# Three shared PSUM bank pairs, neighbour rows worked out on GpSimd, and a one-instruction maximum in a graph and expert kernel

## The chip, the cores and the metric

One core of a Trainium2 chip runs the whole program. The metric is the device time of one execution in microseconds (us). The engines are called as in the profile: PE (TensorE, with its weight loads as PEld), DVE (VectorE), ACT (ScalarE), POOL (GpSimd) and SP (SyncE, which here only issues DMAs).

## What is computed

```python
x = x + gnn(adj, layernorm(x))             # x: 8 x 1024 x 128 f32, adj: 8 x 1024 x 1024 int32
x = x + ffn(layernorm(x), route_id)

def gnn(A, X):                             # S = 25
    scores = where(A != 0, -arange(N), -inf)
    vals, idx = top_k(scores, S)           # the first 25 neighbours of each node
    feats = where(vals > -inf, X[idx], -inf)
    agg = feats.max(axis=2)                # degree <= 25: maximum with 0 too
    return relu(concat([X, agg]) @ W + b)

def ffn(x, route_id):                      # 64 groups of 128 tokens, one of 16 experts for each group
    h = relu(x @ Wi.T + bi)
    for l in range(2):
        h = relu(h @ Ws[l].T + bs[l] + h @ Wr[l, e].T + br[l, e] + h)
    return h @ Wo.T + bo
```

## The kernel before

Each of the 8 batches has 1024 nodes in eight tiles of 128. Tile 0 holds the nodes with the most neighbours (the hubs); it is handled apart. For the seven other tiles (896 target nodes), PE computes for each node how many neighbours came earlier ("rank", L869 and L872, bf16 matmuls of the transposed adjacency with a triangular matrix), ACT copies the rank to SBUF (L641), and then 44 "slots" follow. A slot is a pair (group of source tiles, rank r): an engine makes a one-hot matrix `onehot = (rank == r)` of up to 896 columns (1792 for the group that has two tiles), PE multiplies it with the features (`xsplit`, two parts, L777) into a pair of PSUM banks, and DVE takes the maximum with what is there already (`acc`, a fold, L988; the first two slots of a batch by L986). After 44 folds `acc` holds the maximum over neighbours; L995 merges its two halves.

The slots are numbered p = 0 to 43 in a table. One-hots are shared out by hand: ACT makes 23 of them (by a square and a relu, L670 and L687, or by one relu for r = 1, L681), POOL 16 (L547) and DVE 5 (L975). Six column buffers (`UNITS`) hold them in turn; an engine makes the one-hot of slot p + 5 (ACT, POOL) or p + 4 (DVE) when its own program is at position p, once the buffer's earlier slot has been multiplied.

The program runs in stages s = 0 to 9 of 44 positions, and each engine's instructions are written out by position. In stage s the slots of batch s - 1 run, together with the loading, normalising, mask, transpose and rank work of batch s, and with everything that follows for batch s - 2: the GNN matmuls (p = 2 to 5, L811, L812), the second layer norm (statistics L1169 and norm L1007 to L1018 on DVE, p = 5 to 8; the normalised tile h0 on ACT, L612, p = 9 and 11), turning h0 (PE L819, p = 12 and 13, copied by ACT L618), the first expert matmul (L826, p = 14 to 17), the two expert layers tile by tile (L842 with ACT's relu L629, p = 19 to 34) and the output (L852, p = 36 and 39). In stage 1 the 34 weight matrices are also turned on PE (L908) and summed by DVE (L1153). The steady stages are s = 2 to 7.

PSUM: two pairs of banks for the slots (`slot_ps`), so PE may write slot n when fold n - 2 is done; two single banks for the ranks (`prep_ps`), each used for one half (448 columns) of a rank tile; two single banks (`ffn_ps`) for all that belongs to batch s - 2. The eight ranks of a stage stand at p = 16, 18, 20, 22, 28, 32, 37 and 38.

The hubs: DVE finds each hub's first neighbours by MAX8 and MATCH_REPLACE8 over a `score` row (L1039, L1047, L1049, last at p = 27). At p = 28 DVE turns them into row numbers of a feature table in DRAM (L1057 `spread`, L1058 `floor`, L1061 `idx`); POOL gathers 25 rows for each hub by 25 indirect DMAs (L535), from p = 29 to p = 24 of the next stage; and DVE takes their maximum in two halves of 13 and 12 rows, each in two pieces: one tensor_tensor of six rows with six (p = 14 and 31, L1075 and L1085), and then a chain of four (p = 24 and 34, L1066), with `hub` by L1095.

## Time and profile before

| | |
|---|---|
| median of 3 runs | 740.54 us (737.5 to 740.84) |
| profiled execution | 736.18 us |
| its span in the trace | 734.5 us |
| busy: PE / PEld / DVE | 611.5 / 502.9 / 574.2 us |
| busy: ACT / POOL | 521.2 / 541.9 us |
| granted PE clock, mean | 0.926 of 2.4 GHz |
| chain that ended last | PE 59%, DVE 22%, DMA 4%, ACT 4% |

A batch's first fold (L986) marks the start of its stage: 43.0, 148.0, 225.8, 303.5, 381.5, 459.3, 536.6 and 614.0 us. So stage 1 takes 105 us, the six steady stages some 77.7 us each, the last stage with slots (s = 8) about 76, and the tail some 44. No engine is busy throughout; what has to be read is which of them is waited for at which position of a stage, and that is in the timelines.

### The profile page before, as it was taken

The page shows a single profiled execution, that of the slowest core. Times are in us where ns is not written, and L with a number is a line of the kernel's source. Part 1 is how long each engine was busy: PE and PEld are TensorE (multiplying, and loading weights), DVE is VectorE, ACT ScalarE, POOL GpSimd, SP SyncE. Part 2 cuts the span into 40 slices and gives each one's busy share as a digit, 9 for nine tenths or more (in the row PEclk, how much of TensorE's full clock was granted, in tenths as well). Part 3 has the DMA queues.
Part 4 walks back from the last instruction along what each step waited for, and adds up shares of the span by engine and source line. Part 5 has one row for each costly group of instructions (what it writes and reads, how often), then busy time and mean ns, then how long its engine had stood idle before and what let it go on. Part 6 is the DMA issues. An engine that isn't in the chain of part 4 may idle for free.

```text
span 734.5 us, 11755 instructions
## 1 busy us (share of the span) xinstructions
PE 611.5 (83%) x3496; PEld 502.9 (68%) x3497; DVE 574.2 (78%) x959; ACT 521.2 (71%) x981; POOL 541.9 (74%) x388
## 2 busy tenths in 40 slices
PE   0466666679999799979997999899987999799686
PEld 0054545566987588858885888668875988588565
DVE  3766799878987898779987898789878987777740
ACT  5672455369977898779876987699769985478062
POOL 4577488497979987898878897989799878984000
PEclk9986798898999899979998999989998999799989
DMA  9999997479746965496638755785474543045222
GB/s 298 305 196 265 314 344 241 134 176 293 226 132 158 267 175 152 102 259 205 166 109 222 236 163 142 190 240 159 127 182 124 161 138 87 22 113 144 58 72 77
DMA packets 145171, 131.73 MB, mean 179 GB/s; under 512 B 72219, under 2 KB 112324, under 8 KB 145092
## 3 DMA queue, kind: packets, MB, share of 16 engines
q1 hardware_dynamic: 128124, 105.94, 53.5%
q0 software_dynamic: 7296, 15.74, 8.3%
q10 hardware_dynamic: 9680, 9.21, 4.5%
q8 instruction: 31, 0.51, 0.3%
q14 instruction: 40, 0.33, 0.1%
HBM read 98.20 MB, written 17.98 MB: 158 GB/s over the span
## 4 chain that ended last, share of the span: by engine, by line
PE 59%; DVE 22%; issue 5%; DVEq 4%; DMA 4%; ACT 4%; SPq 1%; ACTq 0%
PE slot_ps L777 28%; PE ffn_ps L842 11%; DVE acc L988 9%; PE ffn_ps L852 4%; PE ffn_ps L826 4%; PE prep_ps L869 3%; DMA at<-mask 2%; PE ffn_ps L811 2%; PE ffn_ps L792 2%; DVEq L1060 2%; DVE top L1047 2%; PE ffn_ps L812 2%; DMA adj_sb<-in_adj_dram 2%; DVE wst L1153 1%; DVE score L1049 1%
## 5 line engine op out<-in xcount | busy, mean ns | idle before, releaser
L777 PE MATMUL slot_ps<-onehot,xsplit 128*128 128x512 f32 (+3 forms) x1376 | 375.5, 401 | 51.1 <-DVE acc L988 44.4
L988 DVE TENSOR_TENSOR acc<-slot_ps,acc 128x896 f32<-128x896 f32 (+2 forms) x336 | 293.7, 884 | 77.3 <-PE slot_ps L777 74.5
L547 POOL TENSOR_SCALAR onehot<-rank,ranks 128x896 fp32r<-128x896 bf16 (+3 forms) x128 | 298.4, 2333 | 72.6 <-PE slot_ps L777 67.5
L777 PEld LDWEIGHTS slot_ps<-onehot,xsplit 128*128 128x128 f32 x1376 | 251.9, 204 | 105.7 <-issue 71.0
L535 POOL DMA_INDIRECT gath<-feature_table,idx x200 | 207.7, 1038 | 47.9 <-issue 42.6
L842 PE MATMUL ffn_ps<-hT,wst 128*128 128x128 f32 x1024 | 135.1, 277 | 0.0
L842 PEld LDWEIGHTS ffn_ps<-hT,wst 128*128 128x128 f32 x1024 | 129.0, 191 | 5.9 <-issue 0.8
L670 ACT ACTIVATE away<-rank,ranks 128x896 bf16<-128x896 bf16 (+4 forms) x136 | 107.9, 793 | 6.8 <-DVE wst L1153 6.4
L687 ACT ACTIVATE onehot<-away 128x896 fp32r<-128x896 bf16 (+4 forms) x136 | 96.3, 708 | 21.5 <-PE slot_ps L777 10.6
L629 ACT ACTIVATE hT<-ffn_ps,wst 128x128 f32<-128x128 f32 x256 | 81.1, 375 | 29.5 <-PE ffn_ps L842 27.3
L641 ACT ACTIVATE rank<-prep_ps 128x448 bf16<-128x448 f32 x128 | 63.0, 550 | 21.0 <-PE prep_ps L869 11.7
L714 ACT ACTIVATE mask<-adj_sb 128x1024 bf16<-128x1024 uint32 x56 | 58.0, 1047 | 25.8 <-DMA at<-mask 20.9
L681 ACT ACTIVATE onehot<-rank,ranks 128x896 fp32r<-128x896 bf16 (+1 forms) x48 | 56.0, 1167 | 22.1 <-PE slot_ps L777 21.3
L869 PE MATMUL prep_ps<-at,before 128*128 128x448 bf16 x128 | 39.9, 380 | 15.0 <-DMA at<-mask 12.3
L908 PE MATMUL ffn_ps<-ident,hT 128*128 128x128 f32 x136 | 26.5, 329 | 28.8 <-DVE wst L1153 25.7
L908 PEld LDWEIGHTS ffn_ps<-ident,hT 128*128 128x128 f32 x136 | 18.8, 169 | 38.8 <-issue 36.7
L1047 DVE MAX8 top<-score 128x8 f32<-128x1024 f32 x32 | 39.0, 1219 | 0.3
L975 DVE TENSOR_SCALAR onehot<-rank,ranks 128x1792 fp32r<-128x1792 bf16 (+2 forms) x40 | 38.5, 962 | 0.7 <-PE slot_ps L777 0.7
L826 PE MATMUL ffn_ps<-xnT,wiT 128*128 128x512 f32 x64 | 33.4, 611 | 0.5 <-ACT xnT L618 0.5
L852 PE MATMUL ffn_ps<-woT,hT 128*128 128x128 f32 x256 | 32.8, 281 | 0.0
L869 PEld LDWEIGHTS prep_ps<-at,before 128*128 128x128 bf16 x128 | 11.4, 99 | 30.9 <-DMA at<-mask 12.4
L852 PEld LDWEIGHTS ffn_ps<-woT,hT 128*128 128x128 f32 x256 | 29.8, 191 | 3.6 <-issue 3.6
(121 smaller groups left out, 586.3 us busy)
## 6 DMA issues: line engine op xcount, KB each, us to landing
wst<-folded_weights SPq DMA_DIRECT2D x128, 257.0 KB, 2.9
adj_sb<-in_adj_dram SPq DMA_DIRECT2D x64, 512.0 KB, 5.9
folded_weights<-wst ACTq DMA_DIRECT2D x34, 256.0 KB, 6.9
hT<-in_L_ffn_Wr_dram SPq DMA_DIRECT2D x26, 256.0 KB, 10.3
xs<-in_x_dram SPq DMA_DIRECT2D x8, 512.0 KB, 8.1
feature_table<-xn SPq DMA_DIRECT2D x8, 512.0 KB, 4.1
x<-in_x_dram SPq DMA_DIRECT2D x8, 512.0 KB, 4.3
out_dram<-h SPq DMA_DIRECT2D x16, 256.0 KB, 2.4
```

The costliest lines, as they stand in the source:

```text
L535: pool.indirect_dma_start(gath[:, j, :], None, tables[b], bass.IndirectOffsetOnAxis(ap=idx[:, b % 2, 0, j:j + 1], axis=0)).then_inc(signal ...
L547: pool.tensor_scalar(onehot[:, UNIT[n]:UNIT[n] + many, 0:wide * P], rank[:, b % 2, first:first + many, 0:wide * P], ranks[:, r - 1:r], Non ...
L629: ins = act.activation(hT[:, 1 - l, j, i, :], ffn_ps[(i + 1) % 2][:, j * P:(j + 1) * P], ACT.Relu, bias=wst[:, i, HC * HID + j:HC * HID + ...
L641: act.activation(rank[:, s % 2, jt, c * CW:(c + 1) * CW], prep_f[c][:, 0:CW], ACT.Copy, bias=float(NONE)).then_inc(s_q, 1)
L670: act.activation(away[:, i % AWAYS, 0:wide * P], rank[:, b % 2, first, 0:wide * P], ACT.Square, bias=ranks[:, r - 1:r], scale=-1.0).then_i ...
L687: act.activation(onehot[:, UNIT[n], 0:wide * P], away[:, i % AWAYS, 0:wide * P], ACT.Relu, bias=1.0, scale=-1.0).then_inc(s_acthot, 1)
L777: mm = pe.matmul(slot_ps[n % 2][:, c0:c1], xsplit[:, b % 2, part, first + j, :], onehot[:, UNIT[n] + j, c0:c1], start=(j == 0 and part == ...
L826: pe.matmul(ffn_ps[1 - j][:, :], wiT[:, j * P:(j + 1) * P], h0T[:, 4 * g:4 * g + 4, :].rearrange("p t c -> p (t c)"), start=True, stop=Tru ...
L842: mm = pe.matmul(ffn_ps[(i + 1) % 2][:, j * P:(j + 1) * P], wst[:, i, c0:c0 + P], hT[:, l, kc, i, :], start=(kc == 0), stop=(kc == HC - 1))
L852: mm = pe.matmul(o, hT[:, 0, kc, i, :], woT[:, kc, :], start=False, stop=(i % 4 == 3 and kc == HC - 1))
L869: mm = pe.matmul(prep_f[c][:, 0:CW], before[:, :], at[:, jt, cols], start=True, stop=not second)
L988: dve.tensor_tensor(acc[:, p % 2, 0:cols], slot_ps[n % 2][:, 0:cols], acc[:, p % 2, 0:cols], ALU.max).then_inc(s_max, 1)
```

## The change

1. The ranks lose their own two banks. There are three pairs of banks, and slots and ranks take them in turn in the order in which PE issues them (`bank_ring`). An item waits for the item three before it: a slot's fold on DVE (`s_max`) or a rank's copy on ACT (`s_q`). A rank is now one pair of matmuls (512 and 384 columns) and one ACT copy of 896 columns, not two of 448.
2. The row numbers are worked out by POOL at p = 30 (p = 17 in stage 0), by four small instructions that wait for each other, in place of three on DVE at p = 28. The gathers move one to two positions later.
3. The maximum of the gathered rows is one tensor_reduce for each half, at p = 14 and p = 31, in place of the tensor_tensor pieces and chains.
4. POOL makes 8 one-hots in place of 16. Slots 12 (384 columns), 27 and 43 (896) go to ACT; 5, 15, 18, 31 (896) and 36 (256) go to DVE.
5. A fold waits for the fold two before it on DVE's own semaphore, which the wait for PE implied so far. The matmuls that turn the small weights at the start use `ffn_ps`.

```diff
@@ constants @@
-CHUNKS = 2
+BANKS = 3
-ACT_HOT = [0, 1, 2, 4, 6, 8, 9, 11, 14, 17, 21, 22, 25, 26, 29, 30, 32, 34, 35, 37, 39, 40, 41]
+ACT_HOT = [0, 1, 2, 4, 6, 8, 9, 11, 12, 14, 17, 21, 22, 25, 26, 27, 29, 30, 32, 34, 35, 37, 39, 40, 41, 43]
-POOL_HOT = [3, 5, 7, 10, 12, 15, 16, 18, 23, 27, 28, 31, 33, 36, 38, 43]
+POOL_HOT = [3, 7, 10, 16, 23, 28, 33, 38]
-    REDUCE_AT = {14: (0, 0, 0), 24: (0, 0, 1), 31: (0, 1, 0), 34: (0, 1, 1)}
-    FIRST_REDUCE_AT = {26: (0, 0, 0), 27: (0, 0, 1), 36: (0, 1, 0), 37: (0, 1, 1)}
+    REDUCE_AT = {14: (0, 0), 31: (0, 1)}
+    FIRST_REDUCE_AT = {26: (0, 0), 36: (0, 1)}
-    GATHER_AT = {29: [0], 30: [1], 32: [2], 33: [3], 35: [4], 36: [5], 38: [6], 39: [7], 41: [8], 42: [9]}
-    GATHER_NEXT = {0: [10], 1: [11], 3: [12], 5: [13], 6: [14], 8: [15], 10: [16], 12: [17], 13: [18],
-                   15: [19], 17: [20], 19: [21], 20: [22], 22: [23], 24: [24]}
+    ROWS_AT = [17, 30]
+    GATHER_AT = {31: [0], 32: [1], 34: [2], 35: [3], 37: [4], 38: [5], 40: [6], 41: [7], 43: [8]}
+    GATHER_NEXT = {0: [9], 2: [10], 3: [11], 5: [12], 7: [13], 8: [14], 10: [15], 12: [16], 13: [17], 15: [18],
+                   17: [19], 18: [20], 20: [21], 22: [22], 23: [23], 25: [24]}
...
-        slot_ps = [pb(f"slot_ps{i}", [P, 2 * BANK]) for i in range(2)]
-        prep_ps = [pb(f"prep_ps{i}", [P, 1024], BF16) for i in range(2)]
+        slot_ps = [pb(f"slot_ps{i}", [P, 2 * BANK]) for i in range(BANKS)]
         ffn_ps = [pb(f"ffn_ps{i}", [P, BANK]) for i in range(2)]
-        prep_f = [p[:, :].bitcast(F32) for p in prep_ps]
...
+        def bank_ring():
+            pair, last, order = {}, {}, []
+            for s, p in positions():
+                if 1 <= s <= B:
+                    order.append(("slot", (s - 1) * NS + p))
+                if s < B and p in RANK_AT[s > 0]:
+                    order.append(("rank", s * IT + RANK_AT[s > 0][p]))
+            for m, item in enumerate(order):
+                pair[item] = m % BANKS
+                last[item] = order[m - BANKS] if m >= BANKS else None
+            return pair, last
+        PAIR, LAST_IN = bank_ring()
...
+            def rows_to_gather(s):
+                pool.wait_ge(s_top, TOPS * (s + 1))
+                if s >= 2:
+                    pool.wait_ge(s_hub, HUBS * (s - 1))
+                pool.tensor_scalar(spread[:, :], top[:, 0, 0:TOPK], 0.0, lane[:, 0:1], ALU.is_equal, ALU.mult
+                                   ).then_inc(s_rows, 1)
+                pool.tensor_scalar(floor[:, s % 2, 0:1], top[:, 0, TOPK:TOPK + 1], 0.0, NEG_BIG, ALU.is_gt, ALU.mult
+                                   ).then_inc(s_rows, 1)
+                pool.wait_ge(s_rows, 4 * s + 2)
+                pool.tensor_tensor(spread[:, :], spread[:, :], top[:, 0, 0:TOPK], ALU.subtract).then_inc(s_rows, 1)
+                pool.wait_ge(s_rows, 4 * s + 3)
+                pool.tensor_scalar(idx[:, s % 2, 0, :], spread[:, :], float(N), None, ALU.add).then_inc(s_rows, 1)
+                pool.wait_ge(s_rows, 4 * s + 4)
...
-                    pool.wait_ge(s_idx, b + 1)
...
+                if s < B and p == ROWS_AT[s > 0]:
+                    rows_to_gather(s)
...
-                    for c in range(CHUNKS):
-                        act.wait_ge(s_rank, 2 * IT * s + 2 * jt + c + 1)
-                        if jt == 0 and c == 0 and s >= 2:
-                            act.wait_ge(s_agg, s - 1)
-                            act.wait_ge(s_cstore[s % 2], 16 * (s // 2))
-                        act.activation(rank[:, s % 2, jt, c * CW:(c + 1) * CW], prep_f[c][:, 0:CW],
-                                       ACT.Copy, bias=float(NONE)).then_inc(s_q, 1)
+                    act.wait_ge(s_rank, IT * s + jt + 1)
+                    if jt == 0 and s >= 2:
+                        act.wait_ge(s_agg, s - 1)
+                        act.wait_ge(s_cstore[s % 2], 16 * (s // 2))
+                    act.activation(rank[:, s % 2, jt, :], slot_ps[PAIR["rank", s * IT + jt]][:, 0:COLS],
+                                   ACT.Copy, bias=float(NONE)).then_inc(s_q, 1)
...
+            def free_pair(item):
+                if LAST_IN[item]:
+                    kind, i = LAST_IN[item]
+                    if kind == "slot":
+                        pe.wait_ge(s_max, i + 1)
+                    else:
+                        pe.wait_ge(s_q, i + 1)
+                return slot_ps[PAIR[item]]
...
-                if n >= 2:
-                    pe.wait_ge(s_max, n - 1)
+                to = free_pair(("slot", n))
...
-                    for c in range(CHUNKS):
-                        if jt == 0:
-                            for i, many in enumerate(turns((s + 1) * TT)):
-                                pe.wait_ge(s_turn[i], 16 * many)
-                            if s > 0:
-                                pe.wait_ge(s_q, 2 * IT * s - 1 + c)
-                        else:
-                            pe.wait_ge(s_q, 2 * IT * s + 2 * jt + c - 1)
-                        cols = slice(c * CW, (c + 1) * CW)
-                        mm = pe.matmul(prep_f[c][:, 0:CW], before[:, :], at[:, jt, cols],
-                                       start=True, stop=not second)
+                    if jt == 0:
+                        for i, many in enumerate(turns((s + 1) * TT)):
+                            pe.wait_ge(s_turn[i], 16 * many)
+                    to = free_pair(("rank", s * IT + jt))
+                    for c0 in range(0, COLS, BANK):
+                        cols = slice(c0, min(c0 + BANK, COLS))
+                        mm = pe.matmul(to[:, cols], before[:, :], at[:, jt, cols], start=True, stop=not second)
                         if second:
-                            mm = pe.matmul(prep_f[c][:, 0:CW], onesb[:, :], at[:, jt - 1, cols],
-                                           start=False, stop=True)
-                        mm.then_inc(s_rank, 1)
+                            mm = pe.matmul(to[:, cols], onesb[:, :], at[:, jt - 1, cols], start=False, stop=True)
+                    mm.then_inc(s_rank, 1)
...
+                if p >= 2:
+                    dve.wait_ge(s_max, n - 1)
...
-            def rows_to_gather(s):
...
-            def larger(to, a, c):
...
-            def reduce_half(b, h, part, piece):
+            def reduce_half(b, h, part):
                 n = b * HUBS + h + 1
-                if part == 0 and piece == 0:
+                if part == 0:
                     dve.wait_ge(s_gathA, 16 * HALF * n)
-                    dve.tensor_tensor(gath[:, 0:6, :], gath[:, 0:6, :], gath[:, 6:12, :], ALU.max
-                                      ).then_inc(s_six, 1)
-                elif part == 0:
-                    dve.wait_ge(s_six, 2 * n - 1)
-                    larger(gath[:, 0:3, :], gath[:, 0:3, :], gath[:, 3:6, :])
-                    larger(gath[:, 0, :], gath[:, 0, :], gath[:, 1, :])
-                    larger(gath[:, 0, :], gath[:, 0, :], gath[:, 2, :])
-                    larger(half_max[:, :], gath[:, 0, :], gath[:, 12, :]).then_inc(s_redA, 1)
-                elif piece == 0:
+                    if n > 1:
+                        dve.wait_ge(s_redB, n - 1)
+                    dve.tensor_reduce(gath[:, TOPK, :], gath[:, 0:HALF, :].rearrange("p k c -> p c k"), AX_X, ALU.max
+                                      ).then_inc(s_redA, 1)
+                else:
                     dve.wait_ge(s_gathB, 16 * (TOPK - HALF) * n)
-                    dve.tensor_tensor(gath[:, 13:19, :], gath[:, 13:19, :], gath[:, 19:25, :], ALU.max
-                                      ).then_inc(s_six, 1)
-                else:
-                    dve.wait_ge(s_six, 2 * n)
-                    larger(gath[:, 13:16, :], gath[:, 13:16, :], gath[:, 16:19, :])
-                    larger(gath[:, 13, :], gath[:, 13, :], gath[:, 14, :])
-                    larger(gath[:, 13, :], gath[:, 13, :], gath[:, 15, :])
-                    larger(half_max[:, :], gath[:, 13, :], half_max[:, :]).then_inc(s_redB, 1)
+                    dve.wait_ge(s_redA, n)
+                    dve.tensor_reduce(half_max[:, :], gath[:, HALF:TOPK + 1, :].rearrange("p k c -> p c k"), AX_X,
+                                      ALU.max).then_inc(s_redB, 1)
+                    dve.wait_ge(s_redB, n)
+                    dve.wait_ge(s_rows, 4 * n)
```

PE, steady stage, positions 16 to 19, before. L777 are the matmuls of slots 17 to 19, L869 ranks 0 and 1, L826 the first expert matmul:

```order
L826 MATMUL ffn_ps1<-xnT,wiT 128x512
L869 MATMUL prep_ps0<-at,before 128x448
L869 MATMUL prep_ps1<-at,before 128x448
L777 MATMUL slot_ps1<-onehot,xsplit 128x512
L777 MATMUL slot_ps1<-onehot,xsplit 128x384
...
L826 MATMUL ffn_ps0<-xnT,wiT 128x512
L777 MATMUL slot_ps0<-onehot,xsplit 128x512
L777 MATMUL slot_ps0<-onehot,xsplit 128x384
...
L869 MATMUL prep_ps0<-at,before 128x448
L869 MATMUL prep_ps1<-at,before 128x448
L777 MATMUL slot_ps1<-onehot,xsplit 128x512
```

And the same place after (L814 the slots, L903 the ranks, L863 the expert matmul):

```order
L863 MATMUL ffn_ps1<-xnT,wiT 128x512
L903 MATMUL slot_ps1<-at,before 128x512
L903 MATMUL slot_ps1<-at,before 128x384
L814 MATMUL slot_ps2<-onehot,xsplit 128x512
L814 MATMUL slot_ps2<-onehot,xsplit 128x384
...
L863 MATMUL ffn_ps0<-xnT,wiT 128x512
L814 MATMUL slot_ps0<-onehot,xsplit 128x512
L814 MATMUL slot_ps0<-onehot,xsplit 128x384
...
L903 MATMUL slot_ps1<-at,before 128x512
L903 MATMUL slot_ps1<-at,before 128x384
L814 MATMUL slot_ps2<-onehot,xsplit 128x512
```

The order is the same; the ranks now stand in a bank pair between those of the slots, so that the slots around them alternate between two pairs.

DVE, steady stage, positions 13 to 17, before: L988 folds, L1047 and L1049 the hub search, L975 one-hots, L1075 the first piece of the maximum:

```order
L988 TENSOR_TENSOR acc<-slot_ps1,acc 128x896
L1047 MAX top<-score 128x8
L988 TENSOR_TENSOR acc<-slot_ps0,acc 128x384
L1075 TENSOR_TENSOR gath<-gath 128x768
L988 TENSOR_TENSOR acc<-slot_ps1,acc 128x896
L975 TENSOR_SCALAR onehot<-rank,ranks 128x1792
L988 TENSOR_TENSOR acc<-slot_ps0,acc 128x896
L975 TENSOR_SCALAR onehot<-rank,ranks 128x2x128
L988 TENSOR_TENSOR acc<-slot_ps1,acc 128x896
```

After (L1022 folds, L1007 one-hots, L1081 the search, L1093 the maximum of 13 rows):

```order
L1022 TENSOR_TENSOR acc<-slot_ps0,acc 128x896
L1081 MAX top<-score 128x8
L1022 TENSOR_TENSOR acc<-slot_ps1,acc 128x384
L1007 TENSOR_SCALAR onehot<-rank,ranks 128x896
L1093 TENSOR_REDUCE gath<-gath 128x128
L1022 TENSOR_TENSOR acc<-slot_ps2,acc 128x896
L1007 TENSOR_SCALAR onehot<-rank,ranks 128x1792
L1022 TENSOR_TENSOR acc<-slot_ps0,acc 128x896
L1007 TENSOR_SCALAR onehot<-rank,ranks 128x2x128
L1022 TENSOR_TENSOR acc<-slot_ps2,acc 128x896
```

Between folds 14 and 15 a one-hot has come in, and the tensor_reduce of 13 rows stands where six rows were compared with six.

DVE, steady stage, positions 27 to 31, before: L1057, L1058 and L1061 are the row numbers, L998 statistics of the next batch:

```order
L1047 MAX top<-score 128x8
L988 TENSOR_TENSOR acc<-slot_ps0,acc 128x128
L1057 TENSOR_SCALAR spread<-top,lane 128x25
L1058 TENSOR_SCALAR floor<-top 128x1
L1061 SCALAR_TENSOR_TENSOR idx<-spread,base,top 128x25
L988 TENSOR_TENSOR acc<-slot_ps1,acc 128x896
L998 BN_STATS stats<-xs 128x6 x2
L988 TENSOR_TENSOR acc<-slot_ps0,acc 128x896
L988 TENSOR_TENSOR acc<-slot_ps1,acc 128x896
L1085 TENSOR_TENSOR gath<-gath 128x768
L988 TENSOR_TENSOR acc<-slot_ps0,acc 128x896
```

After:

```order
L1007 TENSOR_SCALAR onehot<-rank,ranks 128x896
L1081 MAX top<-score 128x8
L1022 TENSOR_TENSOR acc<-slot_ps1,acc 128x128
L1022 TENSOR_TENSOR acc<-slot_ps0,acc 128x896
L1032 BN_STATS stats<-xs 128x6 x2
L1022 TENSOR_TENSOR acc<-slot_ps1,acc 128x896
L1022 TENSOR_TENSOR acc<-slot_ps2,acc 128x896
L1098 TENSOR_REDUCE half_max<-gath 128x128
L1104 TENSOR_SCALAR hub<-half_max,floor 128x128
L1022 TENSOR_TENSOR acc<-slot_ps0,acc 128x896
L1007 TENSOR_SCALAR onehot<-rank,ranks 128x256
```

The row numbers are gone from between folds 28 and 29, a one-hot has come in before fold 28, and the second maximum with `hub` stands as one block behind fold 31.

## Rows read from the trace of the kernel before

**Rows 1.** Stretches: PE, PEld, DVE, ACT, POOL busy (instructions), clock, DMA share, GB/s.
```profile
92.00:148.50 56.50, 38.91 (x202) 29.62 (x201) 51.79 (x79) 28.92 (x40) 39.76 (x28) 0.88 0.74 233
303.50:381.50 78.00, 72.28 (x425) 60.86 (x425) 66.10 (x107) 65.52 (x126) 66.56 (x44) 0.93 0.68 181
614.00:691.00 77.00, 70.52 (x421) 60.17 (x421) 55.04 (x84) 43.53 (x89) 50.90 (x32) 0.93 0.32 87
```

**Rows 2.** Waits, 303.5 to 381.5 us: us in total, times, longest.
```profile
PE slot_ps L777 <- DVE acc L988: 5.6, 6, 2.3
```

**Rows 3.** Timeline of PE: start us, us, what [idle before it, releaser].
```profile
319.34 2.56 PE L777 MATMUL slot_ps<-onehot,xsplit 128*128 128x512 f32 x6 [2.31 <-DVE acc L988]
323.30 0.98 PE L777 MATMUL slot_ps<-onehot,xsplit 128*128 128x384 f32 x2 [1.40 <-DVE acc L988]
...
324.78 3.33 PE L777 MATMUL slot_ps<-onehot,xsplit 128*128 128x512 f32 x8
...
329.04 1.02 PE L826 MATMUL ffn_ps<-xnT,wiT 128*128 128x512 f32 x2
...
358.38 1.05 PE L777 MATMUL slot_ps<-onehot,xsplit 128*128 128x512 f32 x4 [0.67 <-DVE acc L988]
...
379.04 1.04 PE L777 MATMUL slot_ps<-onehot,xsplit 128*128 128x512 f32 x4 [0.45 <-DVE acc L988]
```

**Rows 4.** Timeline of DVE, the same steady stage.
```profile
312.38 1.09 DVE L988 TENSOR_TENSOR acc<-slot_ps,acc 128x896 f32<-128x896 f32 x1 [1.33 <-PE slot_ps L777]
...
320.45 0.17 DVE L1018 SCALAR_TENSOR_TENSOR shift<-mv,rstd 128x16 f32<-128x16 f32 x1
...
328.16 1.09 DVE L988 TENSOR_TENSOR acc<-slot_ps,acc 128x896 f32<-128x896 f32 x1 [3.21 <-PE slot_ps L777]
```

**Rows 5.** Timeline: ACT in that stage, and PE one batch's stage two earlier.
```profile
327.82 0.57 ACT L618 ACTIVATE xnT<-ffn_ps 128x512 f32<-128x512 f32 x1
...
173.63 1.13 PE L826 MATMUL ffn_ps<-xnT,wiT 128*128 128x512 f32 x2 [0.23 <-ACT xnT L618]
```

**Rows 6.** Stretches of 1 us, columns as in rows 1; the clock is third from last.
```profile
318.00:319.00 1.00, 0.00 (x0) 0.00 (x0) 0.97 (x2) 0.76 (x2) 0.96 (x2) 0.68 1.12 359
328.00:329.00 1.00, 1.00 (x7) 1.00 (x6) 0.84 (x1) 1.00 (x2) 0.83 (x2) 0.70 0.97 267
```

**Rows 7.** Timeline: DVE's `spread` and POOL's one-hots beside it.
```profile
351.80 5.05 POOL L547 TENSOR_SCALAR onehot<-rank,ranks 128x896 fp32r<-128x896 bf16 x2
...
354.64 2.25 DVE L1057 TENSOR_SCALAR spread<-top,lane 128x25 f32<-128x25 f32 x1
```

**Rows 8.** Timeline of DVE: the chain of maxima in stages 4 and 1.
```profile
347.38 1.28 DVE L1066 TENSOR_TENSOR gath<-gath 128x384 f32<-128x384 f32 x3
...
112.53 2.63 DVE L1066 TENSOR_TENSOR gath<-gath 128x384 f32<-128x384 f32 x3
```

**Rows 9.** Groups by shape: busy us, mean ns | idle before.
```profile
L1075 DVE TENSOR_TENSOR gath<-gath 128x768 f32<-128x768 f32 x8 | 9.1, 1137 | 0.0
L1194 DVE TENSOR_REDUCE above<-gath 56x1 f32<-56x1152 f32 x1 | 1.3, 1345 | 0.1
L975 DVE TENSOR_SCALAR onehot<-rank,ranks 128x1792 fp32r<-128x1792 bf16 x24 | 29.2, 1218 | 0.0
L687 ACT ACTIVATE onehot<-away 128x896 fp32r<-128x896 bf16 x64 | 61.2, 956 | 7.3 <-PE slot_ps L777 3.3 <-DVE wst L1153 2.3
L641 ACT ACTIVATE rank<-prep_ps 128x448 bf16<-128x448 f32 x128 | 63.0, 550 | 21.0 <-PE prep_ps L869 11.7 <-PE prep_ps L872 7.7 <-DVE wst L1153 1.5
```

**Rows 10.** Timeline: a DVE one-hot within one of POOL's.
```profile
371.53 3.28 POOL L547 TENSOR_SCALAR onehot<-rank,ranks 128x896 fp32r<-128x896 bf16 x1 [2.67 <-PE slot_ps L777]
...
372.88 1.15 DVE L975 TENSOR_SCALAR onehot<-rank,ranks 128x1792 fp32r<-128x1792 bf16 x1
```

**Rows 11.** Timeline of PE in the last stage with slots.
```profile
682.99 3.41 PE L777 MATMUL slot_ps<-onehot,xsplit 128*128 128x512 f32 x16 [0.73 <-DVE acc L988]
```

**Rows 12.** Timeline of ACT: a copy of 512 columns out of PSUM.
```profile
329.13 0.58 ACT L618 ACTIVATE xnT<-ffn_ps 128x512 f32<-128x512 f32 x1
```

62 lines of the change are left out of this document (23 added, 39 removed).

## The prediction

> **What bounds the kernel now.** I read the page first (no engine is busy throughout), then stretches of one stage each, then the waits of a steady stage, and last the timelines of PE, DVE and ACT in it. The stretches [rows 1] say that in a steady stage of 78.0 us PE is busy 72.3 and the three others 65.5 to 66.6: nearly balanced, so only a walk through the stage tells what a saved microsecond is worth. Two further rows mark the exceptions: in stage 1 (92 to 148.5 us) DVE is busy 51.8 of 56.5 us and is the bound, and the last stage with slots takes 77.0 us although DVE has 11 and ACT 22 us less to do. So relief of DVE, ACT or POOL is worth little by itself in a stage; the places where PE waits are what counts.
>
> There are few. PE waited for folds 5.6 us in that stage, in six waits [rows 2], of which the timeline shows four large ones [rows 3]: 2.31 and 1.40 us before slots 10 and 12, 0.67 before slot 31, 0.45 before slot 0 of the next batch. (Slots are found by counting matmuls along the order: 896 columns are four of them.) Elsewhere PE runs without a gap.
>
> The chain goes round like this. PE's slot 5 releases DVE at 312.38 us; from there DVE works without a pause (folds, statistics, norm) to `shift` at 320.45; behind it DVE is so far ahead that it waits 3.21 us for slot 13 [rows 4]. `shift` releases ACT, which makes h0 and then, in its own order, masks, one-hots and xn before it copies xnT, done at 327.82 + 0.57 = 328.39 [rows 5]. PE needs that copy for L826, which it starts at 329.04 [rows 3]. From there PE is full to 357.7 us.
>
> **The third bank pair.** In p = 3 to 14 no rank stands, so a slot may start after fold n - 3, not n - 2. Slot 10 then no longer waits for fold 8; slots 11 to 13 each start one fold earlier. Slot 13 needs fold 10, done at 323.1 (the row of slot 12 starts there, at 323.30), in place of 324.78: 1.5 to 1.7 us earlier. But L826 cannot go before ACT's copy at 328.39, and neither DVE's chain to `shift` nor ACT's after it gets shorter. So of 1.6 us only 329.04 - 328.39 = 0.65 us can be had here. Another stage shows PE already waiting 0.23 us for that copy [rows 5]: there it is 0. The six steady stages lie between these ends; I take 0.35, with 0 and 1.6 (if ACT's chain moved too) as bounds. Before slot 0 no rank stands between slots 41 and 0 either, so the 0.45 goes. Among the ranks (p = 16 to 23) the slots alternate between two pairs and gain nothing; they lose nothing either, for each slot there still waits for fold n - 2 at most, and a rank's copy is in time by several slots.
>
> **The row numbers.** `spread` took 2.25 us, ending with POOL's one-hots (351.80 + 5.05 = 356.85 against 354.64 + 2.25 = 356.89) [rows 7]; with `floor` and `idx`, 354.64 to 357.15, DVE was held 2.5 us before fold 29, and PE's slot 31 waited 0.67 [rows 3]. All of it leaves DVE: 0.67 us. On POOL they are four small ones in place of three, each waiting for the one before. No row shows POOL with 25 columns; its 896 take 5.05 / 2 = 2.5 us, so four cost at most 10 and surely more than nothing. By far the nearer is some 2 us in all, and eight fewer one-hots (six of 2.5 us and two small ones) give POOL 17 us a stage. Behind them wait only the gathers, whose rows are needed half a stage later: nothing.
>
> **The maximum.** Before, a half cost 1.14 us for the six rows [rows 9], then 1.28 for three of the chain and about half a microsecond for the last one [rows 8]: some 2.6 us, 5.2 for both. A tensor_reduce over 1152 contiguous elements took 1345 ns [rows 9], 1.17 ns each; 13 x 128 = 1664 make 1.9 us, 12 rows and the partial result the same. The new one reads with a stride of 512 bytes, which no row shows. Bounds: 1.7 us, and 3.6 for twice the price. I take 1.9, 3.8 for both, since it is the only reduction there is. DVE saves 1.4 us a batch, but the work now stands in blocks at p = 14 and p = 31. At p = 14 DVE gets 1.9 + 0.6 (one-hot 18) in place of 0.9 us: fold 15 ends 1.6 us later against PE, slot 17 starts after it with 0.7 us or more to spare, given that fold 13 came 1.5 us early. At p = 31, fold 32 ends about 362.9 on the old clock and slot 34 wants it at 363.2: just in time. The Trainium skill, "VectorE: DVE Perf Modes", summary of rules, speaks against the edit: tensor_reduce has only the plain mode and is the slowest operation there, to be restructured away. By that rule the old chain should be kept; the reduction's row agrees on one element a cycle, and yet the chain's small pieces add up to more by the rows.
>
> **The moved one-hots.** DVE: 1792 columns took 1.22 us [rows 9], so 896 take 0.6 to 0.7 and 256 about 0.3; four and one make 2.9 us a batch. Against 2.5 + 1.4 saved, DVE comes out 1.0 us lighter. One-hot 5 falls into DVE's pause before fold 3, 15 and 18 into the 3.21 us in front of fold 13 and behind it, 31 and 36 into what the row numbers left. One-hots on ACT: a square and a relu of 896 columns are about 0.96 each [rows 9], so slot 43 costs 1.9, slot 27 1.0, slot 12 (384 columns) 1.0: 3.9 us. A rank was 2 x 0.55 us by the rows, in part overlapped [rows 9]; 512 columns out of PSUM took 0.58 [rows 12], so 896 take about 0.9: 8 x 0.1 to 0.2 = 1 us back. ACT goes from 65.5 to some 68.5 of a stage of 76. Slot 12's falls before `shift`, where ACT is idle; slot 27's uses up the slack of the expert tiles (PE's tile 6 gets its relu with 0.1 to 0.2 us to spare); slot 43's lands where ACT waited for a free buffer. Cover is thin, so I keep 0 to 1 us a stage for ACT in the range.
>
> The Trainium skill, "SBUF — State Buffer", who interferes with whom, says that a VectorE tensor_scalar in a two-port mode and any GpSimd operation exclude each other for a whole instruction. `spread` looks just so [rows 7]. But DVE's one-hot of 1792 columns began at 372.88 within POOL's of 371.53 and took its usual 1.15 us, and POOL's took 3.28 in place of 2.5 [rows 10]: the trace does not bear it out for one-hots. By the row the five new ones cost 2.9 us; by the rule they could wait up to 2.5 each. It is a rival below.
>
> **The sum.** Steady stage: 0.35 + 0.67 + 0.45 = 1.47 us, by six 8.8. Last stage: ACT is light there, so slot 13's 1.6 us count, with 0.45 and the 0.73 before 682.99 [rows 11]: 2.8, taken as 2.5 since the clock is low there. Stage 1: DVE is the bound; in its second half it loses 0.5 (row numbers, unblocked there) and the maxima, which took longer beside POOL (three of the chain 2.63 in place of 1.28 us [rows 8]): 5.2 + 1.4 + some 0.7 in the other half = 7.3, and gets 3.8 and four one-hots, 2.1: net 1.9, and 0.6 of waits for folds: 2.5. Prologue and tail: nothing. Together 13.8 us: the profiled execution's 736.18 would become 722.4. It lies 0.6% below the median of 740.54; on the median the forecast is 740.5 - 13.8 = 726.7.
>
> **Rivals.**
> *The low clock lasts longer* (no change). PE's clock fell to 1.2 GHz at about 318.4 us, after PE had idled before slot 10, and came back to 2.4 at about 328.6, some 4 us after PE had begun to work without a gap [rows 6]. With slot 13 early, PE reaches L826 before ACT's copy and idles about 1 us at 327.3. If the clock then comes back 3 us later, the work of those costs 1.5 us a stage more and eats up the 1.47. Left: 13.8 - 9 = 4.8, less where ACT's new work also delays an expert tile; about 737. The same time comes out if ACT's 3.9 us are the bound.
> *The reduction runs at half rate* (slower). 3.6 us at p = 14 puts fold 16 0.8 us behind slot 18, at p = 31 fold 32 1.5 us behind slot 34: 2.3 - 1.5 = 0.8 us lost a stage, 5 in six; stage 1 loses 3.5 - 2.5, the last stage nothing: 747. It decides from about 2.9 us a reduction. For it: the stride. Against: DVE's rows all go by elements.
> *DVE's one-hots are held* by POOL's, as `spread` was: on average half of 2.5 us, when POOL is in a one-hot (8 x 2.5 of 76 us, one in four): 1.6 us a stage, of which that at p = 14 and 27 reaches PE: 0.5 a stage and 2 in stage 1; 732.
> *ACT's chain shortens as well*, because POOL no longer slows DVE's norm and masks come earlier: the full 1.6 in place of 0.35, 7.5 us more: 718.
>
> **How the numbers follow.** Forecast 0.50 (720 to 733); longer low clock or ACT 0.20 (734 to 741); half rate 0.10 (744 to 751); held one-hots 0.06; ACT shortened 0.14 (713 to 720). Range: 716 to 741, which leaves out the slower case and the best third of the last. About 0.5% is what a measurement can tell from no change, so faster means below 736.8: 0.50 + 0.06 + 0.14 = 0.70; same 0.19; slower 0.11.
>
> **What would show it.** In the changed kernel: PE's waits at slots 10 to 12 shrink by about 1 us in all and a wait for ACT's xnT appears before the first expert matmul, with the distance from `shift` to that copy still 7.9 us; no wait before slots 31 and 0; tensor_reduce near 1.9 us; DVE's new one-hots near 0.65; a stage near 76.2 us; clock low for 6 to 10 us a stage as now. I am wrong if a tensor_reduce takes 3 us, if PE waits at slots 17, 18 or 34, or if the expert tiles wait for ACT.

## The result, and the profile after

| | before | after |
|---|---|---|
| median | 740.7 us (4 runs) | 756.1 us (4 runs) |
| lowest and highest | 737.5 to 741.5 | 750.8 to 758.4 |
| span of the profiled execution | 734.5 us | 755.6 us |

The change makes the kernel slower by a factor of 1.0244, 95% interval 1.0207 to 1.0281; the forecast was 726.7 us with a range of 716 to 741. The experiments below ran at other times, on a kernel before of 735 to 737 us; so they are compared by their ratio to it.

The page of the changed kernel, its busy times and the first shares of its chain:

```profile
PE 607.7 (80%) x3463; PEld 499.4 (66%) x3497; DVE 597.3 (79%) x911; ACT 544.1 (72%) x957; POOL 400.1 (53%) x356
...
PE 51%; DVE 25%; issue 9%; DMA 8%; ACT 4%; SPq 1%; DVEq 1%; ACTq 0%
```

Stretches that answer to [rows 1] (stage 1, a steady stage, the last with slots; columns as there):

```profile
92.00:151.00 59.00, 45.29 (x222) 34.49 (x223) 55.36 (x75) 32.65 (x39) 30.75 (x27) 0.87 0.75 227
311.30:391.10 79.80, 70.56 (x415) 58.60 (x420) 69.40 (x101) 68.16 (x124) 48.80 (x40) 0.96 0.69 177
632.30:712.30 80.00, 72.22 (x419) 60.78 (x419) 60.03 (x83) 46.53 (x94) 33.60 (x25) 0.91 0.31 82
```

POOL is 18 us lighter in this steady stage and the clock is granted for more of it (0.96 against 0.93), yet the stage is longer. DVE is 3.3 us heavier (69.4 against 66.1), where the prediction had it 1.0 lighter. From one batch's first fold to the next, the timelines give 80.4 us as the mean of the six steady stages against 77.7 before; stage 1 took 107.4 (105.0), and what follows the last of these folds 123.3 (120.4). So the loss is 2.7 us in each steady stage, 16 in six, and 5 at the two ends.

The groups by shape that the terms of the sum rest on, as in [rows 9]: DVE's one-hots of 1792 and 896 columns, the two reductions, and ACT's copy of a rank (busy us, mean ns | idle before).

```profile
L1007 DVE TENSOR_SCALAR onehot<-rank,ranks 128x1792 fp32r<-128x1792 bf16 x24 | 30.8, 1283 | 0.0
...
L1007 DVE TENSOR_SCALAR onehot<-rank,ranks 128x896 fp32r<-128x896 bf16 x32 | 27.2, 850 | 0.0
L1098 DVE TENSOR_REDUCE half_max<-gath 128x128 f32<-128x1664 f32 x8 | 24.7, 3093 | 0.0
L1093 DVE TENSOR_REDUCE gath<-gath 128x128 f32<-128x1664 f32 x8 | 24.6, 3069 | 0.0
...
L669 ACT ACTIVATE rank<-slot_ps 128x896 bf16<-128x896 f32 x64 | 58.2, 925 | 38.2 <-PE slot_ps L903 18.0 <-PE slot_ps L905 16.3 <-DVE wst L1162 3.5
```

A reduction takes 3.08 us where the sum had 1.9. DVE's one-hot of 896 columns takes 0.85 us for 0.65, a rank's copy 0.93 for 0.9. The steady stage from 311.3 us on shows what it holds up. The first timeline is DVE's, around p = 14 and p = 31, the second PE's at the slots that wait then (slots 17, 18, 34):

```profile
336.70 0.68 DVE L1007 TENSOR_SCALAR onehot<-rank,ranks 128x896 fp32r<-128x896 bf16 x1
337.30 3.11 DVE L1093 TENSOR_REDUCE gath<-gath 128x128 f32<-128x1664 f32 x1
340.32 1.09 DVE L1022 TENSOR_TENSOR acc<-slot_ps,acc 128x896 f32<-128x896 f32 x1
...
368.01 3.10 DVE L1098 TENSOR_REDUCE half_max<-gath 128x128 f32<-128x1664 f32 x1
371.15 0.29 DVE L1104 TENSOR_SCALAR hub<-half_max,floor 128x128 f32<-128x128 f32 x1
371.36 1.09 DVE L1022 TENSOR_TENSOR acc<-slot_ps,acc 128x896 f32<-128x896 f32 x1
```

```profile
336.42 1.13 PE L863 MATMUL ffn_ps<-xnT,wiT 128*128 128x512 f32 x2 [1.17 <-issue]
...
341.56 1.05 PE L814 MATMUL slot_ps<-onehot,xsplit 128*128 128x512 f32 x4 [0.29 <-DVE acc L1022]
...
343.62 1.05 PE L814 MATMUL slot_ps<-onehot,xsplit 128*128 128x512 f32 x4 [0.16 <-DVE acc L1022]
...
372.59 0.87 PE L814 MATMUL slot_ps<-onehot,xsplit 128*128 128x512 f32 x4 [1.02 <-DVE acc L1022]
```

These are the three waits that the prediction named as the sign of its being wrong. A second loss stands behind them, which it did not name. DVE waits 3.12 us for slot 37, whose four matmuls began at 377.51, and ACT 1.89 us for a rank behind it (the first row is DVE's, then ACT's, then PE's):

```profile
380.26 1.09 DVE L1022 TENSOR_TENSOR acc<-slot_ps,acc 128x896 f32<-128x896 f32 x1 [3.12 <-PE slot_ps L814]
...
380.25 0.92 ACT L669 ACTIVATE rank<-slot_ps 128x896 bf16<-128x896 f32 x1 [1.89 <-PE slot_ps L905]
...
377.51 1.06 PE L814 MATMUL slot_ps<-onehot,xsplit 128*128 128x512 f32 x4
...
381.41 0.55 PE L903 MATMUL slot_ps<-at,before 128*128 128x512 bf16 x2 [1.25 <-DVE acc L1022]
```

By PE's rows slot 37 was done at 377.51 + 1.06 = 378.57 us; DVE and ACT both start 1.7 us later, at the same moment. It is so in every steady stage (1.69 to 1.74 us). I call this the late fold 37. Before the change the same fold starts 0.04 us behind the end of PE's slot (368.79 + 1.06 = 369.85):

```profile
369.89 1.09 DVE L988 TENSOR_TENSOR acc<-slot_ps,acc 128x896 f32<-128x896 f32 x1 [0.62 <-PE slot_ps L777]
...
368.79 1.06 PE L777 MATMUL slot_ps<-onehot,xsplit 128*128 128x512 f32 x4
```

The trace also records when semaphores were updated, and this says where the delay sits. In the changed kernel the update by which PE reports its first output tile (L889, p = 36, just in front of slot 37) is recorded 2.35 to 2.40 us behind the end of that tile's last matmul in each of the six steady stages (in the kernel before 0.01 us). Those of slot 37, of the rank and of slot 38 follow it at distances of 0.06 us. ACT's update that is recorded within one of these delays (at 538.83 us) stands 0.01 us behind the end of its instruction. So it is PE's report that goes out late, in order and from the output tile on; DVE and ACT then react at once. The ends of matmuls are modelled in the profile, so whether PE itself stood still meanwhile is not shown.

### The profile page after: what moved, and what is told of

The parts are those of the page before. It is cut to its first block, busy times and chain, and to the rows that moved or that the text cites. A ratio compares the mean times of both kernels' runs of the same rounds, so it can differ in the third digit from the quotient of the medians.

```text
span 755.6 us, 11924 instructions
## 1 busy us (share of the span) xinstructions
PE 607.7 (80%) x3463; PEld 499.4 (66%) x3497; DVE 597.3 (79%) x911; ACT 544.1 (72%) x957; POOL 400.1 (53%) x356
## 4 chain that ended last, share of the span: by engine, by line
PE 51%; DVE 25%; issue 9%; DMA 8%; ACT 4%; SPq 1%; DVEq 1%; ACTq 0%
PE slot_ps L814 24%; PE ffn_ps L879 12%; DVE acc L1022 11%; DMA at<-mask 5%; PE ffn_ps L889 4%; DVE half_max L1098 3%; DVE onehot L1007 3%; PE ffn_ps L848 2%; PE ffn_ps L829 2%; DMA xs<-in_x_dram 2%; PE slot_ps L903 2%; PE ffn_ps L863 2%; PE ffn_ps L849 2%; ACT h L641 1%; PE ffn_ps L784 1%
## 5 line engine op out<-in xcount | busy, mean ns | idle before, releaser
L814 PE MATMUL slot_ps<-onehot,xsplit 128*128 128x512 f32 (+3 forms) x1376 | 362.9, 395 | 55.3 <-DVE acc L1022 40.2
L1022 DVE TENSOR_TENSOR acc<-slot_ps,acc 128x896 f32<-128x896 f32 (+2 forms) x336 | 294.3, 886 | 80.7 <-PE slot_ps L814 67.7
L814 PEld LDWEIGHTS slot_ps<-onehot,xsplit 128*128 128x128 f32 x1376 | 248.1, 202 | 105.2 <-issue 75.3
L574 POOL TENSOR_SCALAR onehot<-rank,ranks 128x896 fp32r<-128x896 bf16 x64 | 152.0, 2375 | 213.7 <-PE slot_ps L814 208.5
L698 ACT ACTIVATE away<-rank,ranks 128x896 bf16<-128x896 bf16 (+4 forms) x152 | 120.7, 794 | 6.0 <-DVE wst L1162 6.0
L715 ACT ACTIVATE onehot<-away 128x896 fp32r<-128x896 bf16 (+4 forms) x152 | 107.8, 709 | 19.7 <-PE slot_ps L814 9.3
L669 ACT ACTIVATE rank<-slot_ps 128x896 bf16<-128x896 f32 x64 | 58.2, 925 | 38.2 <-PE slot_ps L903 18.0
L1007 DVE TENSOR_SCALAR onehot<-rank,ranks 128x896 fp32r<-128x896 bf16 (+3 forms) x80 | 69.7, 871 | 8.3 <-PE slot_ps L814 8.3
L709 ACT ACTIVATE onehot<-rank,ranks 128x896 fp32r<-128x896 bf16 (+1 forms) x56 | 64.9, 1161 | 11.0 <-PE slot_ps L814 8.9
L903 PE MATMUL slot_ps<-at,before 128*128 128x384 bf16 (+1 forms) x95 | 29.6, 373 | 30.1 <-DMA at<-mask 12.4
L903 PEld LDWEIGHTS slot_ps<-at,before 128*128 128x128 bf16 x128 | 11.1, 102 | 42.8 <-issue 17.4
L1081 DVE MAX8 top<-score 128x8 f32<-128x1024 f32 x32 | 39.1, 1221 | 0.3
L863 PE MATMUL ffn_ps<-xnT,wiT 128*128 128x512 f32 x64 | 34.5, 629 | 3.6 <-ACT xnT L647 2.0
L641 ACT ACTIVATE h<-x,shift,rstd 128x128 f32<-128x128 f32 x64 | 26.2, 481 | 9.8 <-DVE shift L1052 9.8
```

Of the source, the lines that this page charges most:

```text
L574: pool.tensor_scalar(onehot[:, UNIT[n]:UNIT[n] + many, 0:wide * P], rank[:, b % 2, first:first + many, 0:wide * P], ranks[:, r - 1:r], Non ...
L669: act.activation(rank[:, s % 2, jt, :], slot_ps[PAIR["rank", s * IT + jt]][:, 0:COLS], ACT.Copy, bias=float(NONE)).then_inc(s_q, 1)
L698: act.activation(away[:, i % AWAYS, 0:wide * P], rank[:, b % 2, first, 0:wide * P], ACT.Square, bias=ranks[:, r - 1:r], scale=-1.0).then_i ...
L709: act.activation(onehot[:, UNIT[n]:UNIT[n] + many, 0:wide * P], rank[:, b % 2, first:first + many, 0:wide * P], ACT.Relu, bias=ranks[:, 1: ...
L715: act.activation(onehot[:, UNIT[n], 0:wide * P], away[:, i % AWAYS, 0:wide * P], ACT.Relu, bias=1.0, scale=-1.0).then_inc(s_acthot, 1)
L814: mm = pe.matmul(to[:, c0:c1], xsplit[:, b % 2, part, first + j, :], onehot[:, UNIT[n] + j, c0:c1], start=(j == 0 and part == 0), stop=(j ...
```

## The experiments

The theories at the start: **A**, the reduction (longer than forecast, and in two blocks); **B**, the ring (rank 7 and slot 39 wait for folds); **C**, the moved one-hots. Each kernel is the kernel before, the changed kernel or the changed kernel with the old maximum (called the 724-us kernel), with one or two things exchanged. In two of them a maximum is taken over other elements, as their expectations say. Where I give where in a stage time was lost, I compare the starts of PE's slots, counted from the batch's first fold, as means of the six steady stages of the two traces.

**The old maximum put back into the change.**

```diff
-    REDUCE_AT = {14: (0, 0), 31: (0, 1)}
+    REDUCE_AT = {14: (0, 0, 0), 24: (0, 0, 1), 31: (0, 1, 0), 34: (0, 1, 1)}
-   dve.tensor_reduce(...)            # two of 13 rows
+   dve.tensor_tensor(...), larger(...) x4   # twice, in two pieces each, as before
```

> The changed kernel with the old maximum put back: pieces of tensor_tensor at p = 14, 24, 31, 34 (26, 27, 36, 37 in stage 1) in place of two tensor_reduce; the ring of three pairs, POOL's rows and the moved one-hots stay. Theory A, the reduction (3.07 and 3.09 us each in the changed kernel's trace, taken as 1.9 in the prediction, 2.4 us a batch more than forecast and all of it in two blocks): 756 us should come down to 725 to 738, that is by 18 to 31, and PE's waits before slots 17, 18 and 34 go. Theory B, the ring (rank 7 and slot 39 1.4 us late in each steady stage): it still holds that, so 742 to 750. Theory C, the moved one-hots: 745 to 752.

Measured: 724.1 us against 735.8, ratio 0.983 (0.979 to 0.986). So everything but the reduction makes the kernel 1.7% faster, by the ratio 12.8 us on the median of before, where the forecast for the whole change was 13.8. Here are the first folds of two batches in its timeline of DVE, and then its waits of PE between 299.9 and 376.9 us (us in total, times, longest):

```profile
299.90 1.09 DVE L1021 TENSOR_SCALAR acc<-slot_ps 128x896 f32<-128x896 f32 x1
...
376.24 1.09 DVE L1021 TENSOR_SCALAR acc<-slot_ps 128x896 f32<-128x896 f32 x1
```

```profile
PE slot_ps L815 <- DVE acc L1023: 5.3, 4, 2.1
PE ffn_ps L857 <- ACT h L642: 0.2, 1, 0.2
```

The stage takes 76.3 us (the mean of six is 76.2, the figure of the prediction). The four waits stand before slots 10 to 13; there is none at slots 17, 18 and 34, and fold 37 is in time. Against this kernel the changed one loses 4.1 us a steady stage: 1.6 are gone by slot 19 (the first reduction), 2.8 by slot 34 (the second), and 4.1 by slot 39 (the late fold 37).

**The old owners of the one-hots in the change** (`ACT_HOT` and `POOL_HOT` as before).

> The changed kernel with the old owners of the one-hots (POOL 16, DVE 5, ACT 23); the ring, POOL's rows and the tensor_reduce stay. DVE loses 2.9 us or more of work a batch and ACT 3.9. Theory C, the moved one-hots (DVE is the bound in stage 1 and runs 0.85 us for each in place of 0.65; `shift` 0.6 us later beside POOL's one-hot): down from 756 by 12 us or more, to 744 or less. Theory A: by 3 to 8 us, 748 to 753, since the reductions still block folds at p = 14 and 31. Theory B: 752 to 757.

Measured: 758.3 us, ratio 1.028 (1.023 to 1.033): not faster than the change, so C falls, and beyond the branch of A too. Fold 37 is in time here, but DVE's one-hots of 1792 columns took 1.44 us on average for 1.28, and the clock was low for 11.9 us of a stage on average.

**The reductions alone, and the ring alone, in the kernel before.**

> The kernel before with the two tensor_reduce of 13 rows alone in place of the pieces of the maximum. Theory A: before has folds on the path at p = 14 to 18 and p = 31 to 34; two blocks of 3.1 us in place of four of 0.9 to 1.7 cost 2 us a steady stage and as much in stage 1: 752 to 758, most of the loss by themselves. Theories B and C: 741 to 746.

Measured: 759.1 us, ratio 1.033 (1.027 to 1.039). The reductions alone lose at least as much as the whole change does, and here fold 37 is in time.

> The kernel before with the ring of three pairs for slots and ranks alone (one rank, one copy of 896 columns). By the prediction 0.35 + 0.45 us a steady stage, 2.1 in the last and 0.6 in stage 1: 733 to 737. Theory B (ranks 6 and 7 wait for folds 37 and 38, and slot 39 comes 1.4 us late): 741 to 750. Theory A gives the prediction's value; so does C.

Measured: 736.7 us, ratio 1.002 (0.999 to 1.005). No loss, which is against B (the wait of rank 7 in the change is a consequence of the late fold 37), but no gain either. Stage 1 is 5.4 us shorter (99.5), a steady stage 0.7 longer (78.4): PE starts slot 15 1.7 us later than before the change, and at slot 31 makes good 0.9. So the wait before slot 31, which the prediction gave to the row numbers, goes with the ring alone. Its timelines of DVE, POOL and PE in a steady stage, and then a stretch of 1 us of it (columns as in [rows 1]), show what precedes the loss:

```profile
394.90 3.79 DVE L991 TENSOR_SCALAR onehot<-rank,ranks 128x1792 fp32r<-128x1792 bf16 x1
398.61 1.27 DVE L1006 TENSOR_TENSOR acc<-slot_ps,acc 128x896 f32<-128x896 f32 x2
...
395.18 2.56 POOL L560 TENSOR_SCALAR onehot<-rank,ranks 128x896 fp32r<-128x896 bf16 x1
...
399.83 3.32 PE L798 MATMUL slot_ps<-onehot,xsplit 128*128 128x512 f32 x8 [2.42 <-DVE acc L1006]
```

```profile
404.00:405.00 1.00, 1.00 (x4) 0.78 (x3) 1.00 (x2) 0.96 (x3) 1.00 (x1) 0.50 0.96 369
```

With the ring DVE's one-hot of 1792 columns falls beside POOL's of 896 and takes 3.79 us in place of 1.2, ending 0.95 us behind the end of POOL's (so in seven stages); the mean of all rose from 1.22 [rows 9] to 1.95 us. PE then waits 2.42 us before slot 13, and its clock, at 1.2 GHz from 391.8 us on, is still there at 404 to 405 and was low for 13.7 us of this stage; in the 724-us kernel it was low for 6.8 of each. So two of the prediction's rivals, the held one-hots and the longer low clock, are real where the ring comes alone. That they make the whole loss is a reading of this trace; no run separates them.

**The reductions over data as they lie.**

```diff
-   gath[:, 0:HALF, :].rearrange("p k c -> p c k")
+   gath[:, 0:HALF, :].rearrange("p k c -> p (k c)").rearrange("p (c k) -> p c k", k=HALF)
```

> The changed kernel whose two tensor_reduce read the same 1664 elements in the order in which they lie (13 neighbours in a row give one result) in place of 13 rows 512 bytes apart, so the maximum of the hub rows is not the one wanted; all else stays. If the stride alone makes the price: 1664 x 1.17 ns = 1.95 us each, DVE is held 2.3 us a batch less in all, and with two blocks of 2 us the time falls from 756 to 722 to 730, at or below the kernel with the old pieces (724). If tensor_reduce with many short groups costs 3.1 us wherever its data lie: 752 to 758 and 3.1 us each.

Measured: 751.1 us, ratio 1.020 (1.014 to 1.027). By shape:

```profile
L1093 DVE TENSOR_REDUCE gath<-gath 128x128 f32<-128x1664 f32 x8 | 15.0, 1877 | 0.0
```

The stride is the price: 1.88 us for 1664 elements in order, 3.07 for the same number in rows 512 bytes apart. But the time hardly fell, against both branches of the expectation: here fold 37 comes 2.9 us late in every steady stage.

**The old pieces in two blocks.**

```diff
-    REDUCE_AT = {14: (0, 0, 0), 24: (0, 0, 1), 31: (0, 1, 0), 34: (0, 1, 1)}
+    REDUCE_AT = {14: [(0, 0, 0), (0, 0, 1)], 31: [(0, 1, 0), (0, 1, 1)]}
```

> The changed kernel with the old pieces of the maximum (724 us with the pieces at p = 14, 24, 31, 34), but with all pieces of a half in one place, p = 14 and p = 31 (26 and 36 in stage 1). The same DVE work in two blocks of some 3.0 us (0.95 + 0.55 + 3 x 0.3 and the idle between them), hub's 0.3 behind the second: nearly as long as a tensor_reduce of 3.1. If what costs is that DVE is held that long in one place (theory A1): 742 to 754. If it is the total of DVE's work, 1.0 us a batch more by the reductions (theory A2): 724 to 729.

Measured: 750.0 us, ratio 1.016 (1.010 to 1.022), with fold 37 late by 1.3 to 1.5 us. The place matters without any reduction; how much, was settled only when the late fold 37 was gone (below).

**The 724-us kernel without the ring, without the moved one-hots.**

> POOL's rows and the moved one-hots on the kernel before, with its two pairs and its pieces of the maximum (so the 724-us kernel without the ring). By the prediction the ring was worth 0.35 + 0.45 us a steady stage, 2.1 in the last and 0.6 in stage 1, 7.5 in all: 731. If the three parts only work together (the ring alone moved the time by nothing, and the clock stayed low for 10.2 to 13.6 us of each stage against 6.8): 732 to 737.

Measured: 753.9 us, ratio 1.022 (1.015 to 1.028), far outside either branch; fold 37 late by 2.8 to 3.0 us in each of six stages.

> The ring and POOL's rows with the old owners of the one-hots (POOL 16) and the old pieces of the maximum: the 724-us kernel without the moved one-hots. By the prediction the move by itself was worth nothing (DVE +2.9, ACT +3.9 us a batch, POOL -17): 720 to 726. If it is what takes the contention with POOL off DVE (one-hots of 1792 columns took 1.95 us with the ring alone and 1.25 with all three): 731 to 738.

Measured: 729.9 us, ratio 0.993 (0.990 to 0.997), fold 37 in time. The moved one-hots are worth 1.1% once the ring and POOL's rows are there, which is nearer to the second branch: 0.95 us a steady stage, all of it gained by slot 15.

**Pacing the gathers.** In all kernels with a late fold 37 POOL's timeline had the same look; here the changed kernel, around slot 37:

```profile
371.41 1.01 POOL L562 DMA_INDIRECT gath<-feature_table,idx  x1 [0.17 <-issue]
372.73 0.96 POOL L562 DMA_INDIRECT gath<-feature_table,idx  x1 [0.30 <-issue]
373.99 0.94 POOL L562 DMA_INDIRECT gath<-feature_table,idx  x1 [0.30 <-issue]
375.24 0.94 POOL L562 DMA_INDIRECT gath<-feature_table,idx  x1 [0.30 <-issue]
376.49 0.94 POOL L562 DMA_INDIRECT gath<-feature_table,idx  x1 [0.30 <-issue]
377.73 0.94 POOL L562 DMA_INDIRECT gath<-feature_table,idx  x1 [0.30 <-issue]
```

These are six gathers in a row. The 724-us kernel has six as well, though its fold 37 is in time. Before the change one-hots on POOL, which wait for PE, stood between them, so that no more than three came in a row. The next kernels hold them apart by a wait:

```diff
                         for j in where.get(p, []):
+                            if s >= 1 and p >= 31:
+                                pool.wait_ge(s_slot, (s - 1) * NS + p - 1)
```

> The changed kernel in which each of POOL's gathers from p = 31 on first waits for slot p - 2 to be done, so that the six that now stand back to back on POOL (issued every 1.25 us, from 6 us before fold 36 to 1 us behind it) are spread over p = 34 to 43 as they were in the kernel before. Theory G, the burst of gathers: what PE had finished from slot 37 on is seen by DVE and ACT only 3.1 us after fold 36, against 0.6 in the kernel before and in the 724-us one; paced, the gap before fold 37 falls to 0.6 to 1.6 us and the time from 756 to 738 to 746. Theory A1 alone (DVE held in two blocks): the gap before fold 37 stays and so does the time, 754 to 758.

Measured: 745.9 us, ratio 1.015 (1.008 to 1.022). DVE's wait before fold 37 (first row) is 1.54 us and starts 0.1 us behind the end of PE's slot (second row):

```profile
370.04 1.09 DVE L1024 TENSOR_TENSOR acc<-slot_ps,acc 128x896 f32<-128x896 f32 x1 [1.54 <-PE slot_ps L816]
...
368.87 1.06 PE L816 MATMUL slot_ps<-onehot,xsplit 128*128 128x512 f32 x4
```

> The 724-us kernel (the change with the old pieces of the maximum) with the same pacing of the gathers. It has six gathers back to back too but no late fold 37 (0.56 us behind fold 36), so theory G gives nothing here: 722 to 727. Slower by 3 us or more would say that the last gathers of a half then come too late for its maximum.

Measured: 725.2 us, ratio 0.987 (0.982 to 0.991): no difference from 724, as expected. (The pacing does not remove everything: here four gathers still come in a row, and the report of the output tile is recorded 0.9 to 1.0 us late in each steady stage, though fold 37 starts at most 0.3 us behind its slot.)

> POOL's rows and the moved one-hots on two pairs with the old pieces of the maximum (754 us, gap before fold 37 3.5 us), with the gathers paced. Theory G: most of what the ring seemed to be worth there was this gap, six to seven times 2.9 us; 733 to 740. If the gap has another cause: 750 to 756.

Measured: 734.7 us, ratio 0.997 (0.995 to 1.000), from 754. Of the 30 us that the ring seemed to be worth in that company, 19 were the gathers; against the paced kernel with the ring it is worth 1.1%, or 0.8 us a steady stage (76.2 against 77.0), which is the 0.35 + 0.45 of the sum.

> The ring and the moved one-hots with DVE's row numbers and the old pieces of the maximum: the 724-us kernel without POOL's rows. By the prediction they are worth 0.67 us a steady stage and 0.5 in stage 1: 728 to 730. If spread on DVE no longer meets a POOL one-hot, since there are eight fewer (it takes 0.3 us in place of 1.7 to 2.1): 724 to 726. With a late fold 37, as the other kernels have it: 740 or more.

Measured: 751.3 us, ratio 1.024 (1.018 to 1.031), with fold 37 late by 2.0 to 3.5 us: the third branch. The time therefore says nothing of what POOL's rows are worth, but the trace does up to slot 38, where PE is only 0.2 us behind the 724-us kernel. DVE's `spread`, which took 2.25 us before, takes 0.23 where POOL makes eight fewer one-hots:

```profile
359.50 0.23 DVE L1057 TENSOR_SCALAR spread<-top,lane 128x25 f32<-128x25 f32 x1
```

**The reduction again, with the gathers paced.**

> The changed kernel with the two reductions over data as they lie (1.88 us each, the maximum of other elements than wanted) and the gathers paced. It is the change with the price that the prediction took. If blocks of 1.9 us cost nothing, as the prediction had it: 723 to 728. Folds 15 and 16 came 0.9 us later than with the pieces in the unpaced pair of kernels, and caught up by slot 27, so I expect that. If any block costs: 732 or more.

Measured: 725.6 us, ratio 0.986 (0.983 to 0.989). With the price that the prediction took and the gathers held apart, the change is faster by 10.6 us on the median of before, for 13.8 in the forecast. A steady stage takes 76.8 us against 76.2 with the old pieces (paced too). These 0.6 us are lost at slots 17 and 18, none at slot 34. With reductions of 3.08 us another 1.1 are lost at the first place and 1.3 at the second (79.2 us in all).

> The changed kernel with all old pieces of a half in one place (p = 14, p = 31) and the gathers paced. DVE is held 2.9 to 3.3 us in one place at the old price. If the block makes the loss: 738 to 746, as with the reductions (746). If the total of DVE's work does: 725 to 730.

Measured: 742.5 us, ratio 1.010 (1.005 to 1.016). Its block at p = 31 on DVE:

```profile
363.13 0.95 DVE L1109 TENSOR_TENSOR gath<-gath 128x768 f32<-128x768 f32 x1
364.12 1.99 DVE L1090 TENSOR_TENSOR gath<-gath 128x384 f32<-128x384 f32 x3
366.18 0.29 DVE L1090 TENSOR_TENSOR half_max<-gath,half_max 128x128 f32<-128x128 f32 x1
366.82 0.29 DVE L1120 TENSOR_SCALAR hub<-half_max,floor 128x128 f32<-128x128 f32 x1 [0.35 <-issue]
367.03 1.08 DVE L1025 TENSOR_TENSOR acc<-slot_ps,acc 128x896 f32<-128x896 f32 x1
```

DVE is held from 363.1 to 367.0 us, of which 0.7 is because three pieces took 1.99 us here and 1.28 in the kernel with four places. So the work is not quite the same, but of the 17 us that separate it from 725 at least 11 (17 less 8 x 0.7) come from where it stands.

```diff
-   dve.tensor_reduce(gath[:, TOPK, :], gath[:, 0:HALF, :] ...)     # p = 14: 13 rows; p = 31: 13 rows
+   reduced(gath[:, TOPK, :], 0, 7)         # p = 14
+   reduced(gath[:, TOPK + 1, :], 7, 13)    # p = 24
+   reduced(gath[:, TOPK + 2, :], 13, 19)   # p = 31
+   reduced(half_max[:, :], 19, TOPK + 3)   # p = 34
```

> The changed kernel with tensor_reduce in four pieces (7 rows at p = 14, 6 at p = 24, 6 at p = 31, 6 and the three partial maxima at p = 34; 26, 27, 36, 37 in stage 1) and the gathers paced: 28 rows at 0.237 us each = 6.6 us a batch, more than the two reductions (6.2) and 1.4 more than the old pieces, but no piece over 2.2 us. If the block makes the loss: 725 to 732. If the price does: 744 to 750.

Measured: 726.6 us, ratio 0.986 (0.980 to 0.991). Two groups of three by shape:

```profile
L1098 DVE TENSOR_REDUCE gath<-gath 128x128 f32<-128x768 f32 x16 | 24.0, 1503 | 0.0
L1098 DVE TENSOR_REDUCE half_max<-gath 128x128 f32<-128x1152 f32 x8 | 17.4, 2172 | 0.0
```

With the third group (7 rows, 1.74 us) 2 x 1.50 + 1.74 + 2.17 = 6.9 us a batch by strided reductions, more than the change has (6.2), for nearly no loss: the ratio is that of the old pieces, and the steady stage is 0.7 us longer (76.8 against 76.2), again at slots 17 and 18.

**The burst alone.**

```diff
-    GATHER_AT = {29: [0], 30: [1], 32: [2], 33: [3], 35: [4], 36: [5], 38: [6], 39: [7], 41: [8], 42: [9]}
+    GATHER_AT = {29: [0], 30: [1], 32: [2], 34: [3, 4, 5, 6, 7, 8], 42: [9]}
```

> The kernel before with six of the next batch's gathers (rows 3 to 8) issued one behind the other at p = 34, where they used to stand between p = 33 and p = 41. Theory G: the gap before fold 37 goes from 0.6 to 3 us or more in each steady stage and the time from 736 to 748 to 756. If the burst needs something else of the change as well (the later folds, the loads of weights at the same time): the gap stays at 0.6 to 1.6 and the time at 735 to 739.

Measured: 761.4 us, ratio 1.033 (1.027 to 1.039). Gathers moved by a few slots, nothing else, cost some 25 us: fold 37 is 2.3 to 2.6 us late (DVE's row, then PE's), and between folds 39 and 42 another 1.3 us go, for a reason that stays open.

```profile
380.83 1.09 DVE L988 TENSOR_TENSOR acc<-slot_ps,acc 128x896 f32<-128x896 f32 x1 [3.21 <-PE slot_ps L777]
...
377.14 1.06 PE L777 MATMUL slot_ps<-onehot,xsplit 128*128 128x512 f32 x4
```

> The kernel before with four gathers of the next batch (rows 3 to 6) one behind the other at p = 34 and the others at their old places or at p = 41, against six in the run before it (761 us, fold 37 seen 2.6 us late). If it takes more than four in a row: gap before fold 37 0.6 us, 735 to 738. If the delay grows with each gather: gap some 1.5 to 2.5 us, 742 to 752.

Measured: 746.8 us, ratio 1.013 (1.008 to 1.018). Fold 37 is late by 1.0 to 1.3 us. The delay of fold 37 grows from none at three in a row (the kernel before) over 1.3 at four to 2.6 at six. The report of the output tile before it is 1.8 to 2.1 us late with four and 1.7 to 2.0 with six; with six, slot 37's own comes another 1.4 us later.

> The 724-us kernel with its six gathers in a row held until slot 35 is done: they then start some 2.7 us before fold 36 in place of 5.3. If it is spared by the moment: fold 37 or 38 is seen 2 to 3 us late now and the time is 738 to 745. If something else of that kernel spares it: 722 to 728.

Measured: 728.8 us, ratio 0.987 (0.982 to 0.993). The lateness moves with the burst: fold 37 is now 0.6 us late in four stages, and fold 39 is late by 1.6 to 2.3 us in all six. But of that only 1.0 us a stage reaches the end of the stage (77.2 against 76.2 us), since in the ring fold 37 is waited for by rank 7, right behind slot 38, and fold 39 by nothing before slot 42. So the 724-us kernel is spared in part by the moment; why its own six gathers make nothing late at all stays open.

## Why the prediction was wrong

Three things stand between the forecast and the result, in ratios to the kernel before: the changed kernel with reductions of 1.88 us and paced gathers has 0.986, with reductions of 3.08 us 1.015, with the burst as well 1.024. So the change without its two faults gives -11 us, the price of the reductions +22, the burst +7 (the last two within some 6 us by the intervals).

- **The maximum** is the step that failed first. The sum took 1.9 us from the only reduction in the trace [rows 9] and kept 3.6 as the bound; it is 3.08. The row on which the price rested read its elements in order, and the prediction said that no row showed the stride. The Trainium skill, "SBUF — State Buffer", section "Door 1: The DMA port swizzle", says that each access which crosses to a new 16-byte line pays a penalty. By that rule rows 512 bytes apart pay at every element, and the rows agree with it: 1.85 ns for each element in the changed kernel against 1.13 in order. The Trainium skill, "VectorE: DVE Perf Modes", "Rules for kernel authors", which the prediction weighed against this edit, advises to consider restructuring a `tensor_reduce` on a hot path. It decides rightly here, though the four pieces show that what hurt was the length within two blocks.
- **The slack at p = 14 and p = 31** is the step that failed with it. The prediction gave slot 17 "0.7 us or more to spare" at 1.9 us. DVE's pause of 3.21 us before fold 13 [rows 4] is 0.6 to 1.1 us in the change; that the third pair, which makes slot 13 early, had spent the slack in this way is argued and was not run. In the paced kernel with 1.88 us slots 17 and 18 are already up to 0.6 us late against the old pieces. At p = 31 it said "just in time", and that was so. By its own figures for 3.6 us (0.8 and 1.5 us lost) a reduction of 3.08 would lose 0.3 and 1.0; it loses 1.1 and 1.3 beyond the 0.6, about one for one of the 1.2 by which it is longer. Its rival *the reduction runs at half rate* named this mechanism. Its total (747, against 1.015 x 740.7 = 752 with paced gathers) came near by luck, from a price that was too high and a slack that was too large. A chance of 0.10 was too little for a price that no row showed, with the point of decision (2.9 us) well inside the bounds.
- **The row numbers and the moved one-hots** had the sentence that failed next: POOL gets 17 us a stage lighter, "Behind them wait only the gathers, whose rows are needed half a stage later: nothing." Nothing waited too long for a gather. But POOL's one-hots had kept the gathers apart. Lighter, POOL issued six in a row, PE's reports went out late, and DVE and ACT started 1.7 us late at fold 37.
- **The row numbers** also had 0.67 us a stage in the sum, for the wait before slot 31. The ring alone takes that wait away, and with the ring and the moved one-hots there, POOL's rows are worth 0.2 us.
- **The third pair** gave what the sum said, but not in the way it said and not by itself. In the change PE reaches its L863 25.13 us behind the first fold in the stage shown and before it 25.52; the means of six are 24.99 and 25.50, so 0.5 for the 0.35 of the sum. Fold 13 comes 1.4 us earlier in the 724-us kernel. From the end of `shift` to the end of the copy of xnT it is 335.79 + 0.57 - 328.58 = 7.8 us, and 328.39 - 320.62 = 7.8 before (the 7.9 of the prediction counts from the start of `shift`). PE idles 1.17 us there, as said. But PE's waits at slots 10 to 12 did not shrink by 1 us: they are 0.93 + 1.88 + 1.82 = 4.6 us against 2.31 + 1.40 = 3.7, because PE runs further ahead of the folds there. And the ring alone gave nothing; by its timeline, because DVE's large one-hot then fell beside POOL's.
- **The moved one-hots** stood in the sum with nothing. With the ring and the rows in place they bring 1.1%; by the traces, since fewer POOL one-hots meet DVE's (those of 1792 columns take 1.25 us on average against 1.43).
- **The last stage and stage 1**: in the 724-us kernel -2.1 and -0.6 us for -2.5 each. Stage 1 differs by 2 to 7 us, either way, between pairs of kernels that only the pacing tells apart (107.4 and 100.3, 104.4 and 102.1, 99.8 and 105.2), so its term stays unproved.
- That the total of the good parts came out (76.2 us a stage, -12.8 in all for -13.8) is partly luck. Each measured with the other two in place, the ring is worth 0.8 us a stage for 0.8 in the sum, the row numbers 0.2 for 0.67, and the moved one-hots 0.95 for nothing.

Two parts were not run alone, POOL's rows and the moved one-hots.

The change with the old maximum is the better version: 724 us, 1.7% faster than before and, by the two ratios, 4.1% faster than the change.

## What to carry to other kernels

Where two engines walk in step, what an instruction costs is set by how long it holds its engine in one place: in this kernel 6.9 us in four places gave the same ratio as the old pieces (0.7 us a stage by the trace), and 6.2 us in two places cost 22 us in all. Price an operation from a row with the same access pattern, not the same name, and when only a far bound is known, give the case beyond the point of decision its full chance. And when an engine is relieved, look at what its waits were pacing: work behind them moves forward and can collide with something that never waited for it.

## What the runs showed of the hardware

- A `tensor_reduce` over 13 rows 512 bytes apart takes 3.07 us, over the same 1664 elements in order 1.88. In pieces: 1.50 us for 6 rows and 2.17 for 9, or 1.9 to 2.0 ns for each element.
- With four to six indirect gathers issued in a row on POOL, DVE took up finished matmul results of PE late, by 1.0 to 3.5 us in seven kernels and by 0.6 to 2.3 in an eighth, at the same place of every steady stage. With three in a row it did not; with waits between them the delay of fold 37 was 0.3 us at most; and in one kernel six in a row made nothing late. By the recorded semaphore updates it is PE's own that come late (2.35 to 2.40 us behind the matmul's end in the changed kernel, for 0.01), and then in a row 0.06 us apart, while ACT's comes 0.01 us behind its instruction. PE's own rows show no pause meanwhile. What holds the updates up was not found.
- DVE's one-hot beside POOL's can be held until POOL's has ended. In seven stages of the kernel with the ring alone DVE's of 1792 columns starts by its row 0.2 to 0.3 us before one of POOL's of 2.55 us, ends 0.95 us behind it, and takes 3.7 to 3.8 us in place of 1.2. The reverse is [rows 10]: POOL's took 3.28 us in place of 2.5 and ended 0.8 us behind DVE's, which took its usual 1.15. The Trainium skill, "SBUF — State Buffer", "Who interferes with whom", says that whoever issues first has the shared ports for the whole instruction and the other is blocked. Both lengths agree with one of the two being held, so [rows 10] did not speak against the rule for one-hots, as the prediction took it. Who is held cannot be told from the recorded starts: in both cases it is the one that starts first by its row, and in the 724-us kernel (DVE's at 317.60 us, 1.79 us long, beside POOL's from 315.91) it is the later one.
